# A four-layer block with a gated delta rule: the recurrence of a quad begins in mid-period, its last merge level a period later

## The reference

```python
q, k, v = jnp.split(silu(conv4(x @ w_qkv)), ...)   # 16 key heads, 32 value heads, 128 wide
beta = sigmoid(x @ w_b);  g = -(exp(A_log) * softplus(x @ w_a + dt_bias))
q = l2norm(q) * DK ** (-0.5);  k = l2norm(k)
def step(state, inp):
    q_t, k_t, v_t, g_t, b_t = inp
    state = state * jnp.exp(g_t)[:, :, None, None]
    kv_mem = jnp.einsum('bhd,bhde->bhe', k_t, state)
    delta = (v_t - kv_mem) * b_t[:, :, None]
    state = state + jnp.einsum('bhd,bhe->bhde', k_t, delta)
    out_t = jnp.einsum('bhd,bhde->bhe', q_t, state)
    return (state, out_t)
_, outs = jax.lax.scan(step, state0, ...)
rms_inv = rsqrt(mean(core * core, axis=-1) + EPS)
core = norm_w * (core * rms_inv) * silu(x @ w_z)
return core.reshape(Bx, Tx, VALUE_DIM) @ w_out
```

## Time and profile before

| | |
|---|---|
| median of 3 runs | 4808.6 us (4802.09 to 4811.22) |
| the profiled execution | 4772.33 us, its span 4770.4 us |
| busy over the span | PE 83%, DVE 63%, ACT 47%, POOL 42% |
| the stage with the quads | from 1588.9 to 4498.6 us of the span |
| 2000 to 4000 us | PE busy 1768.9, DVE 1405.0, ACT 1036.8, POOL 1343.5 us; granted clock of TensorE 0.93 |

### The profile page before, as it was taken

The page is one execution under the profiler, slowest core; times in us unless marked ns, Lnnn a source line. Parts: engine busy times, 40 slices in busy tenths (PEclk is TensorE's granted clock), DMA queues, the critical chain, the costliest instruction groups (busy, mean ns, idle before and its releaser), DMA issues. The chain is left out here.

```text
span 4770.4 us, 71547 instructions
## 1 busy us (share of the span) xinstructions
PE 3945.3 (83%) x23438; PEld 2510.8 (53%) x23438; DVE 3026.3 (63%) x7155; ACT 2231.8 (47%) x5604; POOL 2010.8 (42%) x4629
## 2 busy tenths in 40 slices
PE   3579999995892588888888988988888888889576
PEld 2323333222551366666666666666666666666444
DVE  4268888862324467677776776776766767767522
ACT  2436666671131345555554554555554555455210
POOL 0000000000203276676676666666667667667200
PEclk7769999995896689999998999999998999999888
DMA  0000000000521101111111111111111111110000
GB/s 27 0 0 1 1 1 1 1 1 3 188 86 48 30 18 33 24 27 32 24 28 30 24 29 30 24 32 26 24 33 26 24 33 26 24 33 18 10 28 18
DMA packets 256235, 127.21 MB, mean 27 GB/s; under 512 B 218514, under 2 KB 240915, under 8 KB 252948
## 3 DMA queue, kind: packets, MB, share of 16 engines
q1 hardware_dynamic: 252820, 114.50, 9.4%
q0 software_dynamic: 3072, 8.39, 0.5%
HBM read 87.22 MB, written 35.39 MB: 26 GB/s over the span
## 5 line engine op out<-in xcount | busy, mean ns | idle before, releaser
L1667 POOL TENSOR_TENSOR dl_blocks_tmp<-dl_blocks_l,dl_blocks_x 128x60 f32<-128x60 f32 (+24 forms) x1984 | 700.2, 353 | 739.1 <-DMA dl_blocks_l<-lm_dram 603.3
L1672 POOL TENSOR_TENSOR dl_blocks_x<-dl_blocks_x,dl_blocks_tmp 128x60 f32<-128x60 f32 (+24 forms) x1984 | 720.8, 363 | 155.4
L550 DVE TENSOR_REDUCE part_max<-mx 128x1 f32<-128x512 f32 x1024 | 636.6, 682 | 80.6 <-PE mx L412 80.5
L1833 DVE SCALAR_TENSOR_TENSOR dl_conv<-dl_raw,dl_weights,dl_conv 128x512 f32<-128x512 f32 x768 | 581.2, 783 | 60.1 <-ACT dl_conv L1601 55.6
L486 ACT ACTIVATE normed_t<-sc 128x1024 f32<-128x1024 f32 x512 | 496.3, 1021 | 221.2 <-PE sc L423 220.9
L1390 PE MATMUL prep<-normed_t,dl_weights 128*128 128x512 f32 x1024 | 536.1, 651 | 17.6 <-DMA dl_weights<-in_w_delta 17.2
L1550 ACT ACTIVATE dl_q_state<-rec_a,t_neg_decay 128x128 f32<-128x128 f32 x512 | 160.5, 364 | 522.4 <-DVE dl_r L1736 522.4
L412 PE MATMUL mx<-k_t,q_t 96*128 96x512 bf16 x1024 | 374.1, 400 | 11.0 <-DVE part_max L550 9.1
L1497 PE MATMUL gate_y_ps<-dl_weights,dl_gated_t 128*128 128x256 f32 x1024 | 322.3, 442 | 34.3 <-ACT dl_gated_t L1556 34.3
L1767 DVE SCALAR_TENSOR_TENSOR dl_gated<-dl_core,dl_out_scale,dl_z_gate 128x128 f32<-128x128 f32 x512 | 174.6, 381 | 256.0 <-POOL dl_out_scale L1705 255.9
L1736 DVE SCALAR_TENSOR_TENSOR dl_r<-rec_a,t_neg_decay,dl_v_scaled 128x128 f32<-128x128 f32 x512 | 155.7, 345 | 243.6 <-PE rec_a L1461 242.9
(11 more groups left out here) (279 smaller groups left out, 8327.2 us busy)
## 6 DMA issues: line engine op xcount, KB each, us to landing
dl_blocks_l<-lm_dram SPq DMA_DIRECT2D x256, 128.0 KB, 2.6
dl_weights<-in_w_delta SPq DMA_DIRECT2D x16, 1032.0 KB, 5.3
lm_dram<-dl_lm SPq DMA_DIRECT2D x256, 32.0 KB, 1.6
xs_dram<-dl_blocks_x SPq DMA_DIRECT2D x256, 32.0 KB, 2.0
dl_inverse_t<-xs_dram SPq DMA_DIRECT2D x256, 32.0 KB, 1.9
rows_dram<-moe_y_rows SPq DMA_DIRECT2D x1, 6016.0 KB, 22.6
moe_x_rows<-rows_dram SPq DMA_DIRECT2D x47, 128.0 KB, 2.2
back_dram<-moe_y_rows SPq DMA_DIRECT2D x47, 128.0 KB, 1.7
```

Source lines behind the costliest of these rows:

```text
L550: dve.reduce_max(part_max[:, t % NT, x[2]:x[2] + 1], bank_of(x)[:, :], AX.X).then_inc(s["ring_read"], 1)
L1667: pool.tensor_tensor(out, L[:, 0:i, i].unsqueeze(1).broadcast_to([P, NM - c0, i]), Xs[:, c0:NM, i:i + 1].broadcast_to([P, NM - c0, i]), AL ...
L1672: pool.tensor_tensor(Xs[:, c0:NM, 0:i], Xs[:, c0:NM, 0:i], out, ALU.add).then_inc(s["solve_step"], 1)
L1833: dve.scalar_tensor_tensor(cv[:, m, :], raw[:, m, k:k + QT_], tap(kh, m, k), cv[:, m, :], ALU.mult, ALU.add).then_inc(s["conv_step"], 1)
```

## The change

**The recurrence moves by half a period.** A new function `chunk_of(n, slot)` gives the chunk of a slot: slots 0 to 7 of period n now hold the last two chunks of quad n-4, and slots 8 to 15 the first two of quad n-3. The fourth quad of a period is called `late` and is still quad n-3.

**The merge moves back.** `turn_blocks` goes from slot 8 to 10, the 32-level to slots 12 and 14 (settled in 13 and 15), and the 64-level into the next period, slots 1 and 4 (settled in 2 and 5). The gate projections `project_z` go to slots 13 and 15; the SiLU of the second moves to slot 0 of the next period. Two steps of the convolution go later, the last to slot 15. `turn_v` goes from slot 5 to 6 and both `scale_v` to slot 7.

**The output of a chunk moves.** `gate` goes from stage 1 of the next chunk to stage 2, behind `new_state`; `turn_gated` from stage 2 to 3; `project_out` from stage 3 to stage 0 of the chunk after; `add_out` from stage 0 to 1 of it.

**GpSimd.** Rows 31 to 12 are now solved in the quad's own period and rows 11 to 1 in the next (before: 31 to 7, and 6 to 1). The four roots stand ahead of `flush_blocks`, ahead of `start_blocks`, ahead of row 22, and at the end. `norm` goes ahead of `gates`.

**Buffers.** `DEPTH` goes from 3 to 4, for keys, queries, attention and the scale tables; `v_scaled` stays three deep. The number of instructions and of bytes moved is the same.

```diff
-DEPTH = 3
+DEPTH = 4
-CONV = {8: [(0, 0)], 9: [(0, 1), (1, 0)], 10: [(0, 2), (1, 1)], 11: [(1, 2), (2, 0)], 12: [(2, 1), (3, 0)],
-        13: [(2, 2), (3, 1)], 14: [(3, 2)]}
+CONV = {8: [(0, 0)], 9: [(0, 1), (1, 0)], 10: [(0, 2), (1, 1)], 11: [(1, 2), (2, 0)], 12: [(2, 1)],
+        13: [(3, 0), (2, 2)], 14: [(3, 1)], 15: [(3, 2)]}
...
-FIRST_ROWS = range(BLK - 1, 6, -1)
-LAST_ROWS = range(6, 0, -1)
-
-ROOT_ROWS = (28, 18)
+FIRST_ROWS = range(BLK - 1, 11, -1)
+LAST_ROWS = range(11, 0, -1)
+
+ROOT_ROW = 22
...
+        def chunk_of(n, slot):
+            return QC * (n - 3) + slot // 4 - QC // 2
...
@@ tensor
-                    g, stage = QC * (n - 3) + slot // 4, slot % 4
+                    g, stage = chunk_of(n, slot), slot % 4
...
-                        if slot == 8:
+                        if slot == 10:
                             turn_blocks(n, merge)
-                        if slot == 10:
+                        if slot == 12:
                             merge32_left(merge)
-                        if slot == 12:
+                        if slot in (13, 15):
+                            project_z(n, merge, (slot - 13) // 2)
+                        if slot == 14:
                             merge32_right(merge)
...
+                    if late is not None:
+                        if slot == 1:
+                            merge64_left(late)
+                        if slot == 4:
+                            merge64_right(late)
@@ gpsimd
                 if merge is not None:
                     for i in LAST_ROWS:
                         solve_row(i)
+                if is_chunk(chunk_of(n, 0)):
+                    root(chunk_of(n, 0))
+                if merge is not None:
                     flush_blocks()
+                if prep is not None:
+                    norm(prep)
                 if front is not None:
                     gates(front)
-                if prep is not None:
-                    norm(prep)
-                if rec is not None:
-                    root(QC * rec)
+                if is_chunk(chunk_of(n, 4)):
+                    root(chunk_of(n, 4))
                 if prep is not None:
                     start_blocks(prep)
                 for i in FIRST_ROWS:
-                    if rec is not None and i in ROOT_ROWS:
-                        root(QC * rec + 1 + ROOT_ROWS.index(i))
+                    if i == ROOT_ROW and is_chunk(chunk_of(n, 8)):
+                        root(chunk_of(n, 8))
                     if prep is not None:
                         solve_row(i)
-                if rec is not None:
-                    root(QC * rec + 3)
+                if is_chunk(chunk_of(n, 12)):
+                    root(chunk_of(n, 12))
@@ vector
+                    if stage == 2 and is_chunk(g):
+                        new_state(g)
+                    if stage == 2 and is_chunk(g - 1):
                         gate(g - 1)
```

79 lines of the change are left out of this document (37 added, 42 removed).

## The result

| | before | after |
|---|---|---|
| median | 4807.6 us (4 runs, 4802.09 to 4811.22) | 4730.5 us (4 runs, 4719.89 to 4738.97) |
| ratio | | 0.9839, 95% interval 0.9817 to 0.9862 |
| profiled execution, its span | 4772.33, 4770.4 us | 4719.89, 4718.0 us |
| flush to flush, 60 middle periods | 44.40 us | 42.97 us |
| first flush to last flush | 2790.3 us | 2700.8 us |

The change makes the kernel 77 us faster. The two profiled executions differ by 52 us only: in that of after the stage began some 26 us later (first flush at 1682.3 us, before at 1656.7), behind work that the change doesn't touch.

What follows compares the result with a forecast made beforehand. The closed loop of POOL's solve and SyncE's DMA was taken as the bound: 44.4 - 0.25 - 1.85 + 0.4 = 42.7 us a period, -104 us over 61 periods, +9 at the end, so 4808.6 - 95 = 4714 us, range 4666 to 4756.

Steps and rivals of the forecast that it cites:

- The loop as bound: POOL's solve, 30.5 us, and the DMA stretch, 13.8 us, form a closed loop that sets the 44.3 us period.
- The wait of the write: SyncE's matrix write waits for VectorE's `lower` about 1.0 us in 18 of 60 periods; removing this gains 0.25 us a period.
- The convolutions: On VectorE beside POOL's solve rows: five fewer of 11 overlapping steps, 0.37 us each, gain 1.85 us a period.
- Line 1797 over rows: Its two VectorE instructions move from the DMA stretch over solve rows 11 to 1, costing 0.4 us a period.
- The sum per period: Flush to flush: 44.4 - 0.25 - 1.85 + 0.4 = 42.7 us, so -1.7 us over 61 periods, -104 us.
- The end: After the last solve's flush, two more chunks than before are still to come, costing +9 us.
- The new waits on GpSimd: Roots ahead of the flush and at slot 15 find operands 2 and 5 us early, so no wait.
- rival 3: Slower: POOL's root ahead of the flush waits for its mean square, delaying DMA; T 45.2, 4867 us; chance 0.10.
- Which waits were to show it: POOL's only long wait stays that for `L`; VectorE's root waits move to slots 14 and 2; PE's for `dl_merge` goes.
- rival 1: The slot stream becomes the bound, T between 43.4 and 44.1 us, 4781 us; chance 0.17.
- Rival 2: The convolutions stay over the solve rows, T about 44.4 us, near 4806 us, no change; chance 0.11.
- Rival 4: Far more gain: two more convolutions outside the solve, no line 1797 cost; T 41.3, 4629 us; chance 0.06.

Runs made afterwards that it cites:

- a_in_solve: Changed kernel with one more GpSimd instruction of 1.08 us per period among the solve rows, behind row 14; ratio 0.9940 to the kernel before.
- a_in_dma: Changed kernel with the same additional 1.08 us GpSimd instruction, but in the DMA stretch behind the gates; ratio 0.9831 to the kernel before.
- a_sp: Changed kernel with SyncE issuing the write of the triangular matrices before it waits for the solved blocks' write; ratio 0.9615 to the kernel before.
- b_root: Kernel before with only the second root moved ahead of `start_blocks`, out of the solve rows; ratio 0.9953 to the kernel before.
- a_turn: Changed kernel with PE's `turn_gated` and ScalarE's `copy_gated` moved behind the other work of their slot; ratio 0.9741 to the kernel before.
- a_no_1797: Changed kernel with the two decay-settling instructions of line 1797 cut from 512 to 4 elements; ratio 0.9820 to the kernel before.
- b_out: Kernel before with only the output chain a stage later and GpSimd's new order, without recurrence shift, later merge or fourth buffers; ratio 0.9862.
- a_more_pe: Changed kernel with one more 512-column matmul ahead of each of four projections, about 1.8 us of PE a period; ratio 0.9893 to the kernel before.
- a_four_conv: Changed kernel with the last four of twelve convolution steps cut from 512 to 4 elements; ratio 0.9614 to the kernel before.
- b_all: b_out with the three further moves of v_all, so without the half-period shift; 4644.7 us, ratio 0.9675 to the kernel before.
- v_all: Changed kernel with the moves of a_sp and a_turn together, and the first root right behind the flush; 4506.1 us, ratio 0.9376 to the kernel before.

## Why the prediction was right, and where its steps were off

Forecast 4714 us, measured 4730.5, 16 us more, inside its own range of 4666 to 4756 (by its own sum T = 42.0 gives 4671, so the lower end was 5 us off). The mechanism held; the number of steps over the solve was mis-sized.

- **The loop as bound** held: a_in_solve, a_in_dma and a_sp show it by adding to it, beside it and taking from it.
- **The wait of the write**, -0.25 us predicted: the DMA stretch is 0.37 us shorter. The direction was right, the cause in part: in all of the 18 periods with 1 us it was line 1797 held by GpSimd's gates, and b_root, where that is in 55 of 60, has the wait in 47. The change mends this too, since the pair now runs elsewhere.
- **The convolutions**: the price per step was right (0.37 against 0.35 measured), their number was not. Six were to be over the solve, 7.5 are: 3.5 fewer, not 5, so -1.3 us and not -1.85. The failed step is the way from slot 2 to slot 10, put at 17 to 18 us. The gate of slot 2 is near where it was expected, F + 32.5 to 35.7 against F + 34.4; from there to the gate of slot 10 it takes 2935.29 - 2916.43 = 18.9 us in the rows above, and 22 us where TensorE's clock is down for 3.4 us of it. The prediction had no term for the clock. Without that low stretch T is 42.7 and 6.4 steps lie over the solve, near the six forecast; the 25 periods with it, 8.9 steps on average, make it 7.5 over all. That part of the miss is a comparison within one trace: no run held the clock up alone. The waits for `rec_a` and `rec_b` lie on that way too, and a_turn shows that the place of `turn_gated`, which the prediction hadn't priced at all, was worth 2.4 of the 6.4 steps. The stream, put at 40.4 us, has less to spare than that.
- **Line 1797 over rows**, +0.4 us predicted, about +0.25 measured by a_no_1797.
- **The sum per period**: -1.7 us predicted, -1.43 measured (0.37 + 1.3 - 0.25), over 61 periods -87 and not -104.
- **The end**, +9 predicted, +10.6 measured. The reason was only half right: b_out, without the half period, has +8.3. At the end one more chunk than before (nine roots and not eight) lies behind the last flush, and not two as the prediction had it; four of them come 7.1 to 10.7 us apart, the last ones 5.5.
- **The new waits on GpSimd**: the root ahead of the flush finds its operand 3.4 to 5.5 us old, where 2 us had been expected, so rival 3, the slower one, had more room than it was given. The root in the DMA stretch waits 2.3 us, which the prediction didn't name and which costs nothing there.
- **Which waits were to show it**: the wait for `L` stayed and that for `dl_merge` went, as said. But VectorE was to wait for roots in slots 14 and 2, and hardly does (31.1 us in all). That was given as the sign of rival 1, a stream that sets the pace, and it isn't one by itself: by a_more_pe the stream is close to the loop's pace without setting it. Rival 2 happened in part, 1.5 steps of it.
- **Rival 4**, far more gain, had the whole length of a step added to the solve. a_four_conv puts a step of 0.750 us at 0.35, so it was rightly held unlikely. The Trainium skill (SBUF — State Buffer, Who interferes with whom) has the second comer blocked for the whole instruction. The traces agree with that, a row of 0.25 us taking 0.80 under a step and line 1797 taking 1.38 us and not 0.42 under the gates of b_root; what failed was the step from there to 0.78 us a convolution, since a row that already runs loses nothing.

## What to carry to other kernels

When two engines wait for each other through a buffer, find the ring (here solve, flush, four DMA trips, first row) and sum its parts; a wait that looks like slack on one engine can be the other half of it. Work on engines outside the ring isn't free: its place in time decides what it lays over the ring, so moving it by a few us, as a_turn did with two lines, can be worth more (47 us) than the shift of the recurrence by half a period (11 us). Look at the matrix engine's granted clock period by period, not only at its mean: here the periods with a low stretch in the wrong place are those with the most work over the ring. Test the parts of a large change alone and again once the bound has moved: the shift was worth 11 us with the long loop and 3% with the short one, and a DMA issued earlier in an in-order queue can delay the one behind it more than it gains.

## What the runs showed of the hardware

- **A convolution step over a chain of short GpSimd instructions** (0.2 to 0.7 us each) lengthens the chain by 0.35 us, under half of its own 0.750: the row that runs when the step begins takes no longer, and the row that begins under it is held until some 0.14 us before the step's end (0.55 us of the 0.69 left, at 2896.08).
- **A VectorE instruction that meets a long GpSimd one** is held the same way: 1.38 us and not 0.42 in b_root, 0.96 longer with 1.10 us of the GpSimd one left. In the kernel after the pair of gates at 2883.01 takes 1.07 and not 0.61 beside the 1.90 us at 2881.77, and the pair at 2027.23 takes 1.92.
- **The elasticity of the loop** wasn't expected: of 1.16 us put in, 0.74 stayed (0.94 between periods without the low stretch of the clock); of 2.3 us taken out of the DMA stretch, 1.86 (1.63).
- **TensorE's granted clock** from 2000 to 4000 us was 0.93 before, 0.94 after, in a_in_solve, in a_in_dma and in b_all, 0.89 in b_root, 0.97 in a_more_pe, a_four_conv, a_sp and a_turn, and 1.00 in v_all. No run shows PE setting one of these periods, but in the kernel after a low stretch of 3.4 us on the stream's way goes with two to three more steps over the solve (8.9 against 6.4), so differences between kernels hold a part that comes by the clock. How large it is in v_all and in b_root is open.
